# Folding a key tile into GpSimd's running sum, in two of the eight sweeps of each graph

## The reference

```python
h = jnp.maximum(_layernorm(x, axis=-1), 0.0)
q, k, v = heads(h @ Wq + bq), heads(h @ Wk + bk), heads(h @ Wv + bv)
scores = jnp.einsum('bhqd,bhkd->bhqk', q, k) * scale
scores = jnp.where(mask[:, None] == 0, -jnp.inf, scores)
attn = jax.nn.softmax(scores, axis=-1)
out = jnp.einsum('bhqk,bhkd->bhqd', attn, v)
x = x + out.transpose(0, 2, 1, 3).reshape(b, s, D_MODEL) @ Wo + bo
```

## Time and profile before

| | us, where nothing else stands |
|---|---|
| median of 3 runs | 1941.29 (1940.07 to 1951.55) |
| the profiled execution | 1939.8 |
| its span, first to last instruction | 1938.0 |
| mean granted clock of TensorE, share of full | 0.995 |
| TensorE busy | 1856.8 (96%) |
| GpSimd busy | 1588.3 (82%) |
| VectorE busy | 1537.6 (79%) |
| ScalarE busy | 1470.7 (76%) |

### The profile page before, as it was taken

One profiled execution on the slowest core, in us unless ns is written; L12 is line 12 of the kernel. 1 busy time (PEld: TensorE's weight loads), 2 busy tenths in 40 slices (PEclk: granted clock), 3 DMA queues, 4 the chain that ended last, 5 costly groups with the idle time before them and its releaser, 6 DMA issues.

```text
span 1938.0 us, 35134 instructions
## 1 busy us (share of the span) xinstructions
PE 1856.8 (96%) x13856; PEld 767.2 (40%) x13856; DVE 1537.6 (79%) x1591; ACT 1470.7 (76%) x1766; POOL 1588.3 (82%) x701
## 2 busy tenths in 40 slices
PE   6799999999999999999999999999999999999997
PEld 3234434344344443444434443334434344343432
DVE  6888876888868877788877888778877788777785
ACT  4678886788867888679886788768887688876763
POOL 0688889888888879879799788888888888898874
PEclk9899999999999999999999999999999999999999
DMA  7512444333625236143351435423344324442121
GB/s 235 141 45 73 123 134 120 106 80 94 162 84 142 71 99 162 57 136 88 115 147 50 126 93 146 116 78 92 109 137 125 88 72 120 127 130 84 43 60 45
DMA packets 114136, 206.09 MB, mean 106 GB/s; under 512 B 12848, under 2 KB 16048, under 8 KB 113968
## 3 DMA queue, kind: packets, MB, share of 16 engines
q1 hardware_dynamic: 113104, 203.47, 37.4%
q10 hardware_dynamic: 864, 0.34, 0.1%
HBM read 153.43 MB, written 50.33 MB: 105 GB/s over the span
## 4 chain that ended last, share of the span: by engine, by line
PE 77%; DVE 10%; issue 4%; DMA 3%; ACT 3%; POOL 2%; SPq 0%; DVEq 0%; POOLq 0%; ACTq 0%
PE ps L775 20%; PE ps L762 19%; PE ps L730 13%; PE ps L812 8%; DVE ring L1059 8%; PE ps L744 7%; PE ps L737 7%; POOL acc L1280 2%; DMA k_stack<-k_parts 1%; ACT ring L895 1%; PE ps L785 1%; DMA k_parts<-k_part 1%; PE ps L726 1%; DVE oT_lo L1116 1%; DVE hT_lo L1068 0%
## 5 line engine op out<-in xcount | busy, mean ns | idle before, releaser
L1059 DVE TENSOR_TENSOR ring<-ps,mask 128x1024 f32<-128x1024 f32 x1024 | 1218.4, 1218 | 329.7 <-PE ps L762 298.8
L895 ACT ACTIVATE ring<-ring 128x1024 f32<-128x1024 f32 x1024 | 1063.1, 1050 | 237.1 <-DVE ring L1059 226.4
L1280 POOL TENSOR_TENSOR acc<-acc,ring 128x1024 f32<-128x1024 f32 x380 | 904.1, 2406 | 0.6 <-ACT ring L895 0.6
L1280 POOL TENSOR_TENSOR acc<-ring 128x1024 f32<-128x1024 f32 x252 | 609.2, 2428 | 311.8 <-ACT ring L895 307.5
L762 PE MATMUL ps<-q_stack,k_stack 128*128 128x512 f16 x2048 | 607.1, 381 | 49.6 <-DVE ring L1059 42.2
L775 PE MATMUL ps<-ring,v_sb 128*32 128x512 f32 x4096 | 506.7, 601 | 0.0
L762 PEld LDWEIGHTS ps<-q_stack,k_stack 128*128 128x128 f16 x2048 | 157.5, 97 | 415.1 <-DVE ring L1059 234.2
L775 PEld LDWEIGHTS ps<-ring,v_sb 128*32 128x32 f32 x4096 | 107.3, 109 | 263.1 <-issue 231.2
L812 PE MATMUL ps<-acc,ones 128*32 128x512 f32 x1008 | 132.5, 597 | 1.1 <-POOL acc L1280 0.9
L923 ACT ACTIVATE rden<-ps 128x512 f32<-128x512 f32 x64 | 38.3, 598 | 119.6 <-PE ps L812 119.6
L737 PE MATMUL ps<-wv_lo,hT_hi 128*128 128x128 f16 x1024 | 100.3, 219 | 0.0
(11 more groups left out here) (88 smaller groups left out, 1543.9 us busy)
## 6 DMA issues: line engine op xcount, KB each, us to landing
x_in<-x SPq DMA_DIRECT2D x172, 256.0 KB, 2.9
edges<-adjT SPq DMA_DIRECT2D x128, 256.0 KB, 3.6
q_stack<-q_parts SPq DMA_DIRECT2D x124, 256.0 KB, 4.7
k_stack<-k_parts SPq DMA_DIRECT2D x124, 256.0 KB, 4.9
q_parts<-q_part SPq DMA_DIRECT2D x64, 256.0 KB, 2.0
k_parts<-k_part SPq DMA_DIRECT2D x64, 256.0 KB, 2.1
out<-x_in SPq DMA_DIRECT2D x60, 256.0 KB, 2.0
ring<-x SPq DMA_DIRECT2D x4, 512.0 KB, 5.5
```

The lines of the kernel that those rows point to most:

```text
L895: nc.scalar.activation(tile, tile, ACT.Exp, scale=SCALE / UP / UP).then_inc(s["prob_ready"], 1)
L1059: nc.vector.tensor_tensor(ring[:, slot_of(kt, pair), :].rearrange("p (a n) -> p a n", n=HALF), ps_s(j), mask[:, kt:kt + 1, half * HALF:(ha ...
L1280: nc.gpsimd.tensor_tensor(acc[:, group, pair, :], first_of, ring[:, slot_of(kt, pair), :], ALU.add).then_inc(s["sum_done"], 1)
```

## The change

In the first sweeps of units 0 and 1 of every graph (16 sweeps), GpSimd also adds key tile 7 to sum B: two adds more per sweep, twelve in place of ten. The term d7 goes in these sweeps, and block 18 becomes p6, p7, dB; dB waits for all twelve sums. The ring tiles of key tile 7 are then given free by GpSimd's sum. The counts of terms and of sums follow.

```diff
+JOINED = {(0, 0), (1, 0)}
+JOINED_BLOCKS = {6: ("p0", "p1"), 10: ("p2", "p3"), 14: ("p4", "p5", "dA"), 18: ("p6", "p7", "dB")}
 
-SUMMED = {1: 0, 2: 2, 3: 4, 5: 6, 6: 8}
-SUMS = 10
-SUMMED_AT = {"A": 6, "B": 10}
+SUMMED = {1: 0, 2: 2, 3: 4, 5: 6, 6: 8, 7: 10}
...
+def joined(V):
+    return V < LAST_SWEEP - 1 and divmod(V % (UNITS * SWEEPS), SWEEPS) in JOINED
...
 def terms_of(V):
-    return LAST_TERMS if V >= LAST_SWEEP - 1 else TERMS
+    return LAST_TERMS if V >= LAST_SWEEP - 1 else "AB" if joined(V) else TERMS
...
-    return BLOCKS if V < LAST_SWEEP - 1 else UNIT_BLOCKS if V < LAST_SWEEP else LAST_BLOCKS
+    return JOINED_BLOCKS if joined(V) else BLOCKS if V < LAST_SWEEP - 1 else UNIT_BLOCKS if V < LAST_SWEEP else LAST_BLOCKS
...
+def summed(V):
+
+    return [kt for kt in SUMMED if kt < 4] if V >= LAST_SWEEP - 1 else [kt for kt in SUMMED if kt < 7 or joined(V)]
...
-    return SUMS * min(V, LAST_SWEEP - 1) + SUMMED_AT["A"] * max(0, V - LAST_SWEEP + 1)
+    return sum(PAIRS * len(summed(W)) for W in range(V))
...
-                    pe.wait_ge(s["sum_done"], sums_before(V) + SUMMED_AT[term])
+                    pe.wait_ge(s["sum_done"], sums_before(V) + (SUMMED[3] + PAIRS if term == "A" else PAIRS * len(summed(V))))
...
-                        if last and up == UNITS - 1 and j % SWEEP // PAIRS >= 4:
-                            continue
-                        if j % SWEEP // PAIRS in SUMMED:
+                        if j % SWEEP // PAIRS in summed(U * SWEEPS + j // SWEEP):
                             sums(U, j, first and up == 0 and j < SWEEP)
```

## The result

| | before | changed |
|---|---|---|
| median of 4 runs, us | 1941.19 (1940.07 to 1951.55) | 1960.99 (1960.53 to 1962.85) |
| span of the profiled execution, us | 1938.0 | 1961.1 |
| mean granted clock | 0.995 | 0.989 |

The changed kernel is slower: ratio 1.0094, 95% interval 1.0072 to 1.0116, +19.8 us. The forecast was 1964.0, +22.7. The time lies within the stated range and at the very edge of the 1% that I had taken as the limit of "no change": the ratio is just inside it, the chances had 0.64 outside. In the changed kernel the lines of the code stand ten further down: the products with ones are L822, GpSimd's sums L1290.

The account below looks back on a forecast made before the run. TensorE, busy for 96% of the span, was taken as the bound. Lists +11.5 us and clock +11.2 us made +22.7, 1939.8 to 1962.5 us on the profiled execution, 1964.0 as median; range 1951 to 1970 us.

Parts of the forecast that it names:

- the chances: Over the whole kernel: 0.64 slower by over about 1%, 0.35 within 1%, 0.01 faster by over 1%.
- Unit 0: Block 18, graphs 1 to 7: dB waits for the twelfth sum, 2.2 us late each, seven times, +15.4 us.
- Unit 1: Block 18, graphs 1 to 7: sums fit with 0.28 us to spare; -0.86 us seven times, -6.0 us.
- Graph 0: Block 18: unit 0 has no wait, -0.86 us; unit 1 has dB wait for the sums, +2.95 us.
- The lists together: Engine lists in all 16 joined sweeps: 15.4 + 2.95 - 0.86 - 6.0 = +11.5 us, without the clock.
- The delay taken whole: Unit 0, graphs 1 to 7: none of the 2.2 us is made good later; bounds 0 and 3.5 us.
- The state argument: Unit 0 after dB's wait: engines resume as before; GpSimd's 1.3 us extra lag is swallowed by its 2.34 us idle.
- Rival C: Unit 0's second sweep makes up TensorE's extra 2.2 us; 1934.4 us, or 1927.5 with all gains; chance 0.05.
- The clock: TensorE idle gaps at dB's waits bring half clock; 1.6 us seven times, +11.2 us, bounds 0 and 13.6.
- Four of four: Trace of before, graph 0: four TensorE gaps of 1.82 to 2.94 us, each followed by half clock for 3.41 us.
- Rival B: TensorE keeps full clock after gaps of 2.9 us; +11.5 to +13 us, 1952.8 to 1954; chance 0.22.
- Rival D: GpSimd's lag spreads: adds meeting VectorE take 3.2 us, or later sweeps wait too; +32 us, 1973; chance 0.10.

Follow-up runs that it names:

- the filled kernels: Changed kernel with 13 and 21 products of zeros ahead of dB in its eight waiting sweeps, run twice: 1954.4 us (ratio 1.0052) and 1954.5 us (1.0057).
- experiment 2: Changed kernel with only the seven first sweeps of unit 0 in graphs 1 to 7 joined; 1965.1 us, ratio 1.0112 against the kernel before.
- experiment 3: Changed kernel with 12 and 17 products of zeros ahead of dB in its eight waiting sweeps; 1954.56, 1954.74, 1964.72 and 1966.06 us, ratio 1.0096.
- 5: Changed kernel with 13 and 21 products of zeros ahead of dB in its eight waiting sweeps; 1954.4 us, ratio 1.0052 against the kernel before.
- 7: Changed kernel with dB and the reciprocal two steps later and 22 other sweeps joined (both of unit 1, first of unit 3); 1968.5 us, ratio 1.0112.
- experiment 8: Changed kernel with key tile 7 left out of the denominator in the 16 sweeps, neither d7 nor the adds; 1930.6 us, ratio 0.9926.
- 10: Kernel with 22 other sweeps joined and dB later, plus one GpSimd wait in unit 2 for VectorE's shift; 1940.4 us, ratio 0.9985.
- 11: Changed kernel as it is, measured and traced a second time beside a filled one on one chip; 1962.5 us, ratio 1.0105.

## Why the prediction was right

**The place and the sign.** GpSimd's share rises from 82 to 85%, and TensorE is still busy for 95%; neither tells of the loss. The race at block 18 told it: what stood at dB's start minus the sums' end. *Unit 0:* 2.23 and 2.2 us were worked out, 2.07 to 2.19 came. *Unit 1:* 0.28 us were to spare, dB didn't wait, and 0.86 us came back seven times. *Graph 0:* -0.8 in unit 0; in unit 1 the list's part was 2.9 against 2.95, with 0.9 more for an add that met VectorE. The lists together made +11.1, or +12.0 with that add, against +11.5, and the filled kernels, which leave that part alone, measured +10.5 and +11.8.

**The delay taken whole.** The state argument held: after the wait GpSimd's idle time swallowed its lag (1.15 us of the 2.34 are left), and the second sweeps of unit 0 are neither longer nor shorter, but for the clock. Rival C falls, by this and by experiment 2.

**The clock** is the term that was mis-sized: "I take 1.6 us seven times, 11.2 us". It was 7.6 us in the profiled execution, 8.0 between changed and filled kernel: fewer gaps were followed (five and four of eight), and a single stretch cost 1.4 us in unit 0, not 1.6; only graph 0's double stretch of 6.8 us cost 2.1. "Four of four" in the kernel before spoke of gaps among thin work, and that was said, but only one gap was taken off for it. Rival B falls: gaps of 2.7 to 2.9 us were followed by half clock 11 times in 21. The Trainium skill, "TensorE: Matmul & The Clock Gate", section "HAM oscillation", warns of longer idle gaps only; these traces disagree with it. Part of the nearness of the total is luck: how many gaps are followed changes from trace to trace, at 1.4 us each, and the 0.9 us of the longer add, which the sum didn't have, made up for some of what the clock fell short.

**Rival D** was priced from an add that meets VectorE, and the sum took no cost for it. It came at one place of sixteen, graph 0, unit 1, and in two ways. In the first trace the new add lost: 3.33 us in place of 2.38, and 0.9 us of wait. In the second VectorE lost, while the adds kept their time:

```profile
134.91 7.04 DVE L1126 SCALAR_TENSOR_TENSOR oT_lo<-o_raw,b_up,oT_hi 128x1024 f16<-128x1024 f32 x1
```

It lay within TensorE's wait there, and the list's part of that place stayed at 2.9 us. Elsewhere the same thing has a far larger price than the 0.8 us per meeting of the prediction: 5 to 9 us where GpSimd has no pause. It took other sweeps and a later reciprocal to bring that out.

**Open.** Why two of the four executions of experiment 3 were 10 us longer. A VectorE instruction kept out for 7 to 9 us would fit: one stood in the traces of experiments 2, 5, 7, 8, 10 and 11, and the execution of experiment 8 that had one outside TensorE's waits took 1941.0 us where its other three took 1927.5 to 1932.5. But the two long executions of experiment 3 weren't profiled. Also open: what decides whether a gap in full work is followed by half clock, and why VectorE is late in unit 1 when dB comes later.

## What to carry to other kernels

To move work onto an engine that is "only 82% busy", don't ask for its share: find the instruction that will wait for the moved work, and subtract the two times there, for each stage and unit by itself. Here the same two adds gave 0.86 us back in one unit and cost 2.2 in another. The order of GpSimd's work puts the difference down to four small bias additions; no run took them out. And a wait on the bounding engine has a second price behind it if it leaves TensorE idle: here 1.4 us for about every second gap near 2.8 us, which made +11 us into +20.

## What the hardware showed beyond that

- A gap of 2.7 to 4.9 us on TensorE in an otherwise full list was followed by 1.2 GHz in place of 2.4 for 3.4 us (once 6.8) 13 times in 23, partly at changing places. Where products of zeros filled the gap, in three traces, none followed.
- GpSimd adds that follow each other without a pause can keep a VectorE instruction with two SBUF inputs out for the whole run, not for one add: 128x8 elements took 5.07 us in place of 0.42, 128x1024 took 7.0 to 9.2 us in place of 1.3 to 3.0, and 128x512 once 8.8 in place of 0.8 to 3.0, each ending within 1.1 us after the run. It is the exception: 11 instructions of this kind in all 14 traces. The Trainium skill, "SBUF — State Buffer", section "SBUF: two separate sides", tells of a lock on the shared ports that the first to start holds for its whole instruction. The lock agrees (an add that began beside a VectorE instruction took 3.33 us in place of 2.38), the extent doesn't: here VectorE stayed out over up to five instructions of GpSimd. One pause of GpSimd per graph, at the right step, was worth 25 us.
